# Query halves of the attention on Pool, and scatters of two parts in groups of four: a cross-attention and mixture-of-experts block on one core

## The reference

```python
x = x + xattn(layernorm(x), ctx)      # 16 heads of 16, q and k layer-normed per head
x = x + ffn(layernorm(x))             # shared gated network + 2 of 8 experts per token

q = layernorm_h(x1 @ Wq.T) * SCALE;  k = layernorm_h(x2 @ Wk.T);  v = x2 @ Wv.T
out = softmax(q @ k.T) @ v;          out = out @ Wp.T + bp

shared = silu(x @ Wg_s) * (x @ Wu_s) @ Wd_s
routed = top-2 experts of sigmoid(x @ W_router) + bias, each (silu(x Wg) * (x Wu)) Wd, weighted
```

## Time and profile before

| what | value |
|---|---|
| time, median of 3 runs | 596.18 us (588.65 to 599.35) |
| the profiled execution | 596.74 us, span of its instructions 594.9 us |
| PE busy | 503.3 us (85% of the span), 2876 matmuls |
| PE weight loads | 290.4 us |
| DVE busy | 344.0 us (58%) |
| ACT busy | 239.1 us (40%) |
| POOL busy | 232.8 us (39%), 206 instructions |
| TensorE clock granted, mean | 0.935 of full speed |
| chain that ended last | PE 50%, DVE 15%, DMA 11%, ACT 8%, issue 7% |

### The profile page before, as it was taken

One profiled execution on the slowest core, in us unless ns is written; L12 is line 12 of the kernel. 1 busy time (PEld: TensorE's weight loads), 2 busy tenths in 40 slices (PEclk: granted clock), 3 DMA queues, 4 the chain that ended last, 5 costly groups with the idle time before them and its releaser, 6 DMA issues.

```text
span 594.9 us, 11013 instructions
## 1 busy us (share of the span) xinstructions
PE 503.3 (85%) x2876; PEld 290.4 (49%) x2877; DVE 344.0 (58%) x1028; ACT 239.1 (40%) x468; POOL 232.8 (39%) x206
## 2 busy tenths in 40 slices
PE   4836879999888888886995979499999999999990
PEld 3734225445444443333542434267667666676660
DVE  5775556776888688536854623145555555555550
ACT  0255778888767767651320011022222222222210
POOL 5354321111111842244073710035665636656644
PEclk9956999999999999887997979799999999999995
DMA  8912911111101320114343545336565656665634
GB/s 272 360 52 77 331 37 36 36 37 36 47 29 46 112 73 37 46 71 127 104 170 125 175 146 151 100 57 111 80 111 94 92 100 93 99 112 82 102 59 45
DMA packets 43766, 60.58 MB, mean 102 GB/s; under 512 B 6512, under 2 KB 34800, under 8 KB 43120
## 3 DMA queue, kind: packets, MB, share of 16 engines
q1 hardware_dynamic: 28688, 36.92, 20.4%
q0 software_dynamic: 15040, 23.21, 20.1%
HBM read 33.77 MB, written 29.52 MB: 106 GB/s over the span
## 4 chain that ended last, share of the span: by engine, by line
PE 50%; DVE 15%; DMA 11%; ACT 8%; issue 7%; another core or an unknown queue 5%; POOLq 1%; POOL 1%; SPq 1%; DVEq 0%; ACTq 0%
PE bankS L979 11%; DMA out<-VR,attn 9%; PE bankS L995 7%; PE bankV L871 6%; PE bankS L1029 4%; PE bankQ L746 3%; PE bankR L746 3%; ACT attn L627 3%; PE bankV L875 2%; PE bankS L858 1%; PE bankS L1042 1%; PE bankS L1045 1%; PE bankS L846 1%; POOLq L532 1%
## 5 line engine op out<-in xcount | busy, mean ns | idle before, releaser
L535 POOL DMA_INDIRECT out<-VR,attn x72 | 111.2, 1544 | 133.1 <-DVE VR L1451 84.2
L979 PE MATMUL bankS<-experts,scores_in 128*128 x288 | 104.9, 497 | 1.8 <-issue 0.6
L489 POOL DMA_INDIRECT sorted_rows<-XR,route x64 | 63.6, 993 | 82.3 <-DVE XR L1310 27.2
L627 ACT ACTIVATE attn<-bankS,bias 128x512 f32<-128x512 f32 x128 | 81.1, 682 | 11.4 <-PE bankS L846 11.3
L995 PE MATMUL bankS<-experts,scores_in 96*128 x288 | 74.3, 380 | 0.8 <-DVE scores_in L1442 0.8
L979 PEld LDWEIGHTS bankS<-experts,scores_in 128*128 128x128 f32 x288 | 52.4, 192 | 34.0 <-issue 9.8
L711 ACT ACTIVATE scores_in<-bankS 128x192 f32<-128x192 f32 x72 | 23.8, 331 | 110.9 <-PE bankS L979 103.2
L871 PE MATMUL bankV<-attn,VS 128*32 128x512 f32 x256 | 64.0, 623 | 5.0 <-DVE OTT L1217 3.7
L873 PE MATMUL bankD<-attn,ON 128*32 128x512 f32 x256 | 64.0, 622 | 0.0
L1436 DVE TENSOR_TENSOR scores_in<-scores_in,bankS 128x192 f32<-128x192 f32 x72 | 25.4, 354 | 51.5 <-ACT scores_in L711 39.4
L429 POOL DMA_DIRECT2D x_in<-in_xT x13 | 9.6, 736 | 112.0 <-PE bankQ L746 111.0
(11 more groups left out here) (249 smaller groups left out, 866.8 us busy)
## 6 DMA issues: line engine op xcount, KB each, us to landing
VS<-sorted_rows SPq DMA_DIRECT2D x72, 130.0 KB
x_cols<-X2T SPq DMA_DIRECT2D x16, 256.0 KB, 2.2
scores_in<-x_cols SPq DMA_DIRECT2D x16, 256.0 KB, 3.1
out<-X SPq DMA_DIRECT2D x8, 512.0 KB
x_in<-in_xT POOLq DMA_DIRECT2D x15, 256.0 KB, 3.1
experts<-in_wgu SPq DMA_DIRECT2D x2, 1536.0 KB, 9.7
X<-in_x SPq DMA_DIRECT2D x1, 2048.0 KB, 16.6
experts<-in_wd SPq DMA_DIRECT2D x2, 768.0 KB, 16.3
```

The lines of the kernel that those rows point to most:

```text
L489: pool.indirect_dma_start(sorted_rows.rearrange("s p r -> (s p) r"), bass.IndirectOffsetOnAxis(ap=index, axis=0), rows, None, bounds_check ...
L535: pool.indirect_dma_start(out, bass.IndirectOffsetOnAxis(ap=dest[:, i:i + 1], axis=0), y_out[:, i % 4], None, bounds_check=B * N + SPARE - ...
L627: act.activation(Pb[:, u % 2, c, :], bankS[:, c % GH, :], ACT.Exp, bias=bias[:, b, GH * g + c:GH * g + c + 1] if c < GH else biasR[:, b, g ...
L979: last = pe.matmul(gate_bank(k)[:, 0:2 * F], x_col[:, k, c * P:(c + 1) * P], rhs, start=(c == 0), stop=(c == KC - 1))
```

## The change

For pieces 3 to 15 Pool makes both float16 halves, in a new function `halves_of` that stands right behind the bias addition of the same piece: a copy with a cast to the high half, and a subtraction for the low half, each with a semaphore of its own. ACT's `high` and DVE's low half are left out for these pieces, and who waited for them waits for `q_low`. The load of x moves from piece m + 4 to piece m + 2, behind the halves. Before every fourth scatter of parts three and four, Pool waits until all scatters issued so far have landed (`landed`).

```diff
+            def landed():
+                for s in scat:
+                    pool.wait_ge(s, 16 * (n_scat[0] // 4))
...
+            def halves_of(n):
+                hi, lo = (qs[:, :, :, :, l, :].rearrange("p t g j d -> p (t g j) d") for l in range(2))
+                nq_h = nq[:, :, :, :, :].rearrange("p t g j d -> p (t g j) d")
+                pool.wait_ge(nq_ready, n + 1)
+                pool.wait_ge(qt_ready, n)
+                pool.tensor_copy(hi, nq_h).then_inc(q_high, 1)
+                pool.wait_ge(q_high, n + 1 - EARLY)
+                pool.tensor_tensor(lo, nq_h, hi, ALU.subtract).then_inc(q_low, 1)
+
             for m in range(PIECES):
                 biased(m)
-                n = m + EARLY + 1
-                if m >= 1 and n < PIECES:
+                if m >= EARLY:
+                    halves_of(m)
+                n = m + 2
+                if m >= EARLY and n < PIECES:
                     load(n)
                 if m >= PIECES - 5 and m < PIECES - 1:
                     pool.wait_ge(placed, 1)
...
             for j in range(2 * PT):
+                if j % 4 == 0:
+                    landed()
                 scattered(2, j)
...
             for j in range(2 * PT):
+                if j % 4 == 0:
+                    landed()
                 scattered(3, j)
...
             def root(n):
                 act.wait_ge(qv_ready, n + 1)
-                if n >= 2:
+                if n >= 2 and n - 1 <= EARLY:
                     act.wait_ge(qs_ready, n - 1)
+                if n - 1 > EARLY:
+                    act.wait_ge(q_low, n - 1 - EARLY)
...
                             exps(u, (1,))
-                            high(pc)
...
             def turned_queries(n):
-                pe.wait_ge(qs_ready, n + 1)
+                if n < EARLY:
+                    pe.wait_ge(qs_ready, n + 1)
+                else:
+                    pe.wait_ge(q_low, n + 1 - EARLY)
...
                 hi, lo = (qs[:, :, :, :, l, :].rearrange("p t g j d -> p (t g j) d") for l in range(2))
-                dve.wait_ge(q_hi, n + 1)
-                dve.tensor_tensor(lo, nq_h, hi, ALU.subtract).then_inc(qs_ready, 1)
+                if n < EARLY:
+                    dve.wait_ge(q_hi, n + 1)
+                    dve.tensor_tensor(lo, nq_h, hi, ALU.subtract).then_inc(qs_ready, 1)
```

More of the change, by code:

```diff
@@ L236, in build @@
         q_hi = sem("q_hi")
+        q_low = sem("q_low")
+        q_high = sem("q_high")
         nq_ready = sem("nq_ready")
@@ L543, in square @@
                 act.wait_ge(u_ready, n + 1)
-                if n >= 2:
+                if n >= 2 and n <= EARLY:
                     act.wait_ge(qs_ready, n)
+                if n > EARLY:
+                    act.wait_ge(q_low, n - EARLY)
                 act.activation(squares(n), q_bank(n), ACT.Square).then_inc(sq_ready, 1)
@@ L1139, in queries @@
                 dve.wait_ge(qr_ready, n + 1)
-                if n >= 1:
+                if n >= 1 and n <= EARLY:
                     dve.wait_ge(qs_ready, n)
+                if n > EARLY:
+                    dve.wait_ge(q_low, n - EARLY)
                 nq_h = nq[:, :, :, :, :].rearrange("p t g j d -> p (t g j) d")
```

## The result

The changed kernel takes 617.21 us (median of 4 runs, 615.76 to 618.73) and the kernel before 594.71 us (median of 4 runs beside it, 588.65 to 599.35): ratio 1.041, 95% interval 1.032 to 1.051, slower. The profiled execution took 616.07 us against 596.74, so the two traces differ by 19.3 us of the 22.5 between the medians. Some executions of any kernel here are some per cent slower at a lower clock; medians are of all runs, ratios and intervals leave those executions out.

What follows compares the result with a forecast made beforehand. PE was taken as nearly full in attention, with late signals stretching the shared network. 10.0 + 1.8 + 11.0 + 6.6 + 8.8 - 16 = +22.2 us on 596.74 gives 618.9, or 618 from the median of 596.18; range 603 to 636.

Steps and rivals of the forecast that it cites:

- Piece 3: Attention, piece 3: its halves queue behind Pool's late first addition and three more; PE waits 12.0 us, net +10.0.
- Pieces 5 to 11: Regular attention pairs: Pool's halves come 0.25 us late for PE, seven times, +1.8 us.
- Piece 12: Attention, piece 12: its halves queue on Pool behind four scatters that wait for part one's placing, +11.0 us.
- Pieces 13 to 15: Last attention pieces: halves 4.0 us late behind scatters waiting for weighted values, pairs of 16.7 us, together +6.6 us.
- Clock: PE at low clock behind its waits: 2.6 us for each of two long ones, 1.2 for three short, +8.8.
- C: Rival, attention: PE's clock holds through the waits and DVE's regained time fills the short ones; 603 us, chance 0.12.
- Fours: Shared network: scatters of parts three and four in groups of four end PE's late signals, -16 us.
- Rival B: Shared network: late signals stay, from scatters in any grouping or SP's stores beside them; 634 us, chance 0.25.
- The price of a landing: Pool's seven new waits beside the shared network: about 1.4 us each, 10 in all, hidden.
- rival F: Shared network: landings slow at 4.4 us a wait, Pool ends 10 us behind the network; 628 us, chance 0.06.
- The Trainium skill's rule on the shared port pair: Attention: Pool's passes lock DVE's small routing operations out, some 8 us, not held in the sum.

Runs made afterwards that it cites:

- the early addition: The changed kernel with one addition of 1 element on Pool ahead of its waits for piece 2's rows: 614.05 us, against 616.48 for the changed kernel.
- third batch: The last group of follow-up runs, in which the kernel before took 593.95 us (median of 12 runs).
- second batch: The middle group of follow-up runs, in which the kernel before took 599.65 us (median of 13 runs).
- first batch: The earliest group of follow-up runs, in which the kernel before took 579.96 us (median of 13 runs).
- both repairs: The changed kernel with piece 3's halves on ACT and DVE again and part one's scatters one piece later: 587.01 us.
- the early addition on the kernel before: The kernel before with the landing waits at every fourth scatter and one addition of 1 element on Pool ahead of piece 2's waits: 581.70 us, ratio 0.980.

## Why the prediction was right

It was 618.0 us, within 603 to 636; 617.21 came. That the two meet to 0.8 us is luck in part: for the profiled execution it said 618.9, and 616.07 came. By its steps, from the two traces:

1. **Piece 3**, +10.0 net of 2.0 that returns, PE waiting 12.0. PE waited 12.31, and piece 4 is 11.3 us late, clock included, where the sum had 10.0 and 2.6 of clock: 1.3 less, of which 1.1 is that this trace was that much ahead before piece 3. Taking the piece away from Pool gave back 15.1 us, where the step and its clock stood for 12.6. The traces of that pair have piece 5 12.9 us earlier and the network 14.1, so the step was about right, and the rest lies in pieces behind it. That Pool's start is fixed was right: the experiment with the early addition moved it only together with the instruction of the other kind.

2. **Pieces 5 to 11**, +1.8. From piece 4 to piece 11 the delay grew from 11.3 to 12.2, +0.9. A regular pair is 12.80 us in place of 12.67. The prices of Pool's passes were a little high, by the view of groups:

```profile
L513 POOL TENSOR_TENSOR qs<-nq,qs 128x512 f16<-128x512 f32 x13 | 15.0, 1153 | 1.0
L511 POOL CAST qs<-nq 128x512 f16<-128x512 f32 x13 | 8.0, 613 | 2.7 <-DVE nq L1174 2.7
```

0.61 for the copy, 0.70 taken; 1.15 for the subtraction, 1.15 taken. The lower row (half of 1.122, 0.56) was the nearer one. The 769 ns that the Trainium skill gives in GPSIMD Engine Reference, section 3.1, are not confirmed by either pass.

3. **Piece 12**, +11.0. It came 26.09 us behind piece 11 (25 expected) and added 11.5, against the +11.0 of the sum. With the scatters behind the halves it comes 14.84 us behind it.

4. **Pieces 13 to 15**, +6.6, pairs of 16.7 us. The pairs are 18.66, 19.47 and 18.21 us and added 12.8. The waits are as worked out (3.95 for 4.0). The 2.0, 2.8 and 1.5 us on top are what step 5 counts apart as clock. Up to the turn of piece 15 the steps have 6.6, and 2.6 behind piece 12's wait, and 1.2 twice behind the waits of pieces 13 and 14: 11.6, so 1.2 too little. The kinds of loss are the ones named; that all of the 2.0, 2.8 and 1.5 is clock is not shown.

5. **Clock**, +8.8. Half clock stood behind both long waits and all three short ones. If half of PE's busy time in the five stretches shown above was lost, they cost 2.4, 2.2, 3.1, 1.7 and 3.1 us: the two long waits are near the 2.6 taken, the short ones were mis-sized at 1.2 each. The kernel before stands at half clock in the attention too, for 3.4 us each from 248.3 and from 262.0, which the sum left out. Some 12.5 less 3.4 is 9.1, so the total is met because the two errors balance. The rival in which the short waits leave the clock alone and DVE's time fills them (C, 603 us) had its test at the turn of piece 13: under 14.1 us. It was 18.66.

6. **Fours**, -16. 100.8 us became 84.3: -16.5. Shown to be the fours by giving them to the kernel before (583.90 against 593.95 in the third batch, and a network of 84.4 us where the trace with SyncE's stores moved has 101.2) and by taking them away from the changed kernel: 632.25 and 100.6 in that batch, against 617.21 and 84.3 with them in the result, and 616.48 and 83.5 in the second batch; both times the kernel before had a long network. Rival B (634 us) had the signals late in any grouping: it falls. What it describes is what the changed kernel takes without the fours, 632.25. The price of a landing was mis-sized: 1.4 us taken from a plain write. By the view of waits:

```profile
POOL sorted_rows L491 <- DMA sorted_rows<-XR,route: 23.9, 9, 5.0
```

The seven waits in front of a four took 2.4 to 5.0 us each, 3.3 on average. Pool's last scatter began at 394.17 and landed 2.59 us later, at 396.8, while DVE ended the network at 395.95, so the landing was not hidden: the chain that ended last runs through these scatters, with 4% of the span in their landings and 4% in Pool's line 491. It uncovered next to nothing, since without the fours the network was no shorter (84.0 against 84.3), and in the second trace of the changed kernel the chain runs through the network. The point from which a landing would cost, 2.9 us a wait, was put about right, and rival F (628 us), which took 4.4 a wait, lay nearer than its 0.06 says.

The Trainium skill's rule on the shared port pair (SBUF — State Buffer, SBUF: two separate sides) would have added 8 us in DVE's routing. Single operations of DVE did get slower beside Pool's passes, one line of the routing for example, before and after:

```profile
L1267 DVE TENSOR_TENSOR route<-route 128x64 f32<-128x64 f32 x8 | 1.8, 219 | 0.1
```

```profile
L1299 DVE TENSOR_TENSOR route<-route 128x64 f32<-128x64 f32 x8 | 3.3, 411 | 0.1
```

Two of the eight carry it, the others take 0.21 to 0.28 us. One begins at 176.77, takes 1.22 us and ends 0.09 us behind Pool's addition of 176.62 to 177.90; one begins at 263.01, takes 0.69 and ends 0.09 us behind Pool's copy of 262.99 to 263.61. So the trace agrees with the rule in kind, but in this line it is 1.5 us, and no piece became late by it: with the scatters moved, pieces 13 and 14 have no wait at all.

By the traces: 36.1 us of attention (predicted 38.2 with its clock) less 16.5 (16) is 19.6 (22.2); the medians differ by 22.5. The prediction took the kernel before as a fixed 596, though. In an hour like that of the first batch, where nothing is late in the kernel before, its -16 would have been nothing and the loss some 37 us: the changed kernel without the fours measured 1.064 there. The changed kernel itself was not run in such an hour.

No run shows a gain from the halves on Pool. In the first batch the changed kernel with its scatters moved has 1.020 (1.013 to 1.028) and with piece 3 given back 1.037 (1.030 to 1.044), where the fours alone have 1.001. With both repairs the ratio to before is 0.985 (0.973 to 0.996), with the fours alone 0.975 (0.965 to 0.985), but in different batches and with intervals that overlap, so these two can't be told apart. A regular pair is no shorter with the halves on Pool (12.80 for 12.67 us): the work taken from DVE and ACT was not on the path from one turn to the next.

## What to carry to other kernels

Before work moves to an idle engine, read the order of that engine and not its busy time: here 1.8 us of new work for each of 13 pieces cost 36 us, because it queued behind four scatters that wait for a later result and behind a first addition that starts late; putting the same scatters behind the work gave back 26 us of the time. Two opposite edits in one change should be tried apart, since the fours alone gained 2.5% in one batch and nothing in another, where the whole change lost 4%. And where the time of the old kernel has two levels, take its trace at both before crediting an edit with the difference.

## What the runs showed of the hardware

While Pool issued sixteen scatters in a row, ACT idled for 12 to 16 us, where 4.7 to 6.4 are usual in the short networks, on signals of matmuls that PE had long issued, and the profile mostly named no releaser ("remote"); with a wait for landing ahead of every fourth scatter this is gone (84 us for the network in place of 101 to 104). It appeared in traces of two batches and in the one of the result, and not in the one trace without the fours of the first batch, whose program had it in the third. Moving SyncE's stores changed nothing (101.2 us).

The first addition on Pool behind its copies of float16, where the trace has a change of Pool's program, starts behind 9.6 us of idling with one element and 10.9 to 12.2 with 512. An indirect scatter of one of these row blocks kept the next four waiting 2.4 to 5.0 us for its landing, where a plain write of 130 KB took 2.4 us from issue to landing. And TensorE's granted clock fell to half at all three waits of 3.95 us; at the same wait of piece 4 it held through 2.38 us in the trace of the kernel before and fell in that of the fours alone (2.37 us, 0.79 between 76 and 84 us) and in that with the early addition on the kernel before (1.92 us, 0.79), so the length of a wait alone did not decide it. It also fell where PE waited for no half: for 3.4 us each from 219.5 and from 236.6 in the second trace of the kernel before.
